# Loading two weight matrices in two halves each, in a linear-attention and mixture layer on eight cores

## What is computed

```python
xn = layernorm(x)
# attention branch: linear attention with decay, 8 heads of 64
q, k = phi(xn @ W_Q.T), phi(xn @ W_K.T)          # phi(u) = elu(u) + 1
v    = xn @ W_V.T
S = g*S + outer(k_t, v_t);  z = g*z + k_t        # scan over 2048 steps
y = (S.T q_t) / (z.q_t + eps) * sigmoid(xn @ W_g_w.T + W_g_b)
# other branch: a linear layer and two of eight rank-4 adapters by softmax weight
base = xn @ W_lin.T + b_lin
lora = sum over top-2 e of score_e * (xn @ left_e) @ right_e
out  = x + y @ W_O.T + base + lora
```

## Time and profile before

| What | us |
|---|---|
| Median of the timed runs (2 runs, 416.75 and 417.91) | 417.33 |
| The profiled execution: its time | 418.39 |
| The profiled execution: span of its slowest core, core 7 | 417.3 |
| Busy on core 7: TensorE matmuls | 311.7 |
| Busy on core 7: VectorE | 204.0 |
| Busy on core 7: ScalarE | 131.2 |
| Busy on core 7: GpSimd | 24.6 |

### The profile page before, as it was taken

One profiled execution on the slowest core, in us unless ns is written; L12 is line 12 of the kernel. 1 busy time (PEld: TensorE's weight loads), 2 busy tenths in 40 slices (PEclk: granted clock), 3 DMA queues, 4 the chain that ended last, 5 costly groups with the idle time before them and its releaser, 6 DMA issues.

```text
span 417.3 us, 6496 instructions; the slowest of 8 cores (407.2 to 417.3 us)
## 1 busy us (share of the span) xinstructions
PE 311.7 (75%) x2066; PEld 142.6 (34%) x2066; DVE 204.0 (49%) x807; ACT 131.2 (31%) x281; POOL 24.6 (6%) x64
## 2 busy tenths in 40 slices
PE   0002797417999989368999987379999896799966
PEld 0002342202344534233444443224444444244421
DVE  5040175205267616364665456455575276555741
ACT  1827133474143224416225234150223141401100
POOL 0910000210000000120000000200000002000000
PEclk9999998665699999759999999589999996799977
DMA  7999998000033321000320110001011100010111
GB/s 197 230 211 154 155 164 138 2 0 1 0 103 102 101 61 41 2 1 2 101 87 20 49 52 0 3 0 49 2 53 52 50 1 2 0 52 2 50 52 50
DMA packets 12850, 24.95 MB, mean 60 GB/s; under 512 B 2929, under 2 KB 7153, under 8 KB 12818
## 3 DMA queue, kind: packets, MB, share of 16 engines
q0 software_dynamic: 7856, 7.49, 12.9%
q1 hardware_dynamic: 4242, 14.43, 10.5%
q10 hardware_dynamic: 720, 2.62, 2.0%
HBM read 23.63 MB, written 8.39 MB: 77 GB/s over the span
## 4 chain that ended last, share of the span: by engine, by line
PE 65%; ACT 10%; DVE 9%; issue 7%; POOL 6%; DMA 2%; DVEq 1%; ACTq 0%; SPq 0%; POOLq 0%
PE pQK L786 15%; PE pG L584 8%; PE pQK L799 8%; PE pQK L400 7%; PE pA L400 4%; PE pG L400 3%; PE pV L572 3%; PE pQK L790 3%; PE pT L340 2%; PE pQK L793 2%; ACT gsig L591 2%; DMA crow_s<-crow 2%; PE pO L572 2%; ACT scr1b L286 2%; DVE A_sb L628 2%
## 5 line engine op out<-in xcount | busy, mean ns | idle before, releaser
L786 PE MATMUL pQK<-wlin_sb,xnfm 128*128 128x512 bf16 x256 | 66.1, 405 | 4.8 <-DVE th_sb L557 4.7
L808 DVE TENSOR_TENSOR out_sb<-pQK,x_sb 128x512 f32<-128x512 f32 x32 | 22.1, 692 | 78.6 <-PE pQK L799 75.0
L584 PE MATMUL pG<-wg_sb,xnfm 128*128 128x512 bf16 x128 | 36.0, 432 | 17.1 <-DVE den_r L729 16.2
L591 ACT ACTIVATE gsig<-pG 128x512 bf16<-128x512 f32 x16 | 9.6, 598 | 100.6 <-PE pG L588 100.6
L786 PEld LDWEIGHTS pQK<-wlin_sb,xnfm 128*128 128x128 bf16 x256 | 24.9, 103 | 33.9 <-issue 12.4
L799 PE MATMUL pQK<-wo_sb,ygfm 128*128 128x512 bf16 x128 | 34.9, 397 | 0.0
L415 ACT ACTIVATE phir<-phiw 128x512 bf16<-128x512 f32 x32 | 19.9, 630 | 33.0 <-DVE phiw L409 33.0
L737 DVE SCALAR_TENSOR_TENSOR ygtm<-gsig,den_r,pA 128x64 bf16<-128x64 bf16 x128 | 26.0, 276 | 4.4 <-issue 3.8
L584 PEld LDWEIGHTS pG<-wg_sb,xnfm 128*128 128x128 bf16 x128 | 13.2, 106 | 37.4 <-issue 25.9
L628 DVE TENSOR_TENSOR A_sb<-pA,masks 128x128 bf16<-128x128 f32 x64 | 17.9, 280 | 11.0 <-PE pG L615 11.0
L340 PE MATMUL pT<-ident_s,xn_tm 128*128 128x128 bf16 x128 | 10.9, 241 | 15.0 <-ACT xn_tm L325 12.9
(11 more groups left out here) (144 smaller groups left out, 507.3 us busy)
## 6 DMA issues: line engine op xcount, KB each, us to landing
out<-out_sb SPq DMA_DIRECT2D x16, 512.0 KB, 2.7
x_sb<-x SPq DMA_DIRECT2D x11, 512.0 KB, 5.7
x_sb<-x ACTq DMA_DIRECT2D x5, 512.0 KB, 11.5
wlin_sb<-wlin POOLq DMA_DIRECT2D x1, 2048.0 KB, 49.4
wq_sb<-wq POOLq DMA_DIRECT2D x1, 1024.0 KB, 19.9
wk_sb<-wk POOLq DMA_DIRECT2D x1, 1024.0 KB, 26.4
wv_sb<-wv POOLq DMA_DIRECT2D x1, 1024.0 KB, 32.0
wg_sb<-wg POOLq DMA_DIRECT2D x1, 1024.0 KB, 37.1
```

Of the source, the lines that this page charges most:

```text
L584: TE.matmul(pG[:, :], xnfm[:, 1024 * k + cs * 128 : 1024 * k + cs * 128 + 128], wg_sb[:, FH * k : FH * k + FH], start=(k == 0), stop=False)
L786: TE.matmul(pQK[bank][:, :], xnfm[:, 1024 * k + cs * 128 : 1024 * k + cs * 128 + 128], wlin_sb[:, D * k + 512 * n : D * k + 512 * n + 512] ...
L808: ins = VE.tensor_tensor(out_sb[:, cp * D + 512 * n : cp * D + 512 * n + 512], pQK[bank][:, :], x_sb[:, cx * D + 512 * n : cx * D + 512 * ...
```

## The change

The DMAs of `wv` and `wg` are each issued as two DMAs of four slabs. The second halves have semaphores of their own, "v2" and "g2". In `E_vg` TensorE waits for these before the matmul of k = 4, in every call.

```diff
-    s_wg = {g: nc.alloc_semaphore(f"s_w_{g}") for g in ["qk", "k2", "v", "g", "lg", "ow", "wo2"]}
+    s_wg = {g: nc.alloc_semaphore(f"s_w_{g}")
+            for g in ["qk", "k2", "v", "v2", "g", "g2", "lg", "ow", "wo2"]}
...
-            (wq_sb, wq_d, "qk"), (wk_sb, wk_d, "k2"), (wv_sb, wv_d, "v"),
-            (wg_sb, wg_d, "g"), (wlin_sb, wlin_d, "ow"), (wo_sb, wo_d, "wo2")]
+            (wq_sb, wq_d, "qk", None), (wk_sb, wk_d, "k2", None),
+            (wv_sb, wv_d, "v", "v2"), (wg_sb, wg_d, "g", "g2"),
+            (wlin_sb, wlin_d, "ow", None), (wo_sb, wo_d, "wo2", None)]
...
+        else:
+            h_ = kk // 2
+            dv = dst[:, :].rearrange("p (k c) -> p k c", k=kk)
+            sv = srcd.rearrange("k p c -> p k c")
+            GP.dma_start(dv[:, 0:h_, :], sv[:, 0:h_, :]).then_inc(s_wg[grp], 16)
+            GP.dma_start(dv[:, h_:kk, :], sv[:, h_:kk, :]).then_inc(s_wg[grp2], 16)
+            w_tot[grp] += 16
+            w_tot[grp2] += 16
...
         for k in range(KCH):
+            if k == KCH // 2:
+                TE.wait_ge(s_wg["v2"], w_tot["v2"])
             ins = TE.matmul(pVb[:, :],
...
         for k in range(KCH):
+            if k == KCH // 2:
+                TE.wait_ge(s_wg["g2"], w_tot["g2"])
             TE.matmul(pG[:, :],
```

More of the change, by code:

```diff
@@ L175, in build_core @@
                                      ALU.subtract))
-    wmap = [(gatew_sb, gatew_d, "lg"), (left_sb, left_d, "lg"),
-            (wq_sb, wq_d, "qk"), (wk_sb, wk_d, "k2"), (wv_sb, wv_d, "v"),
-            (wg_sb, wg_d, "g"), (wlin_sb, wlin_d, "ow"), (wo_sb, wo_d, "wo2")]
+    wmap = [(gatew_sb, gatew_d, "lg", None), (left_sb, left_d, "lg", None),
+            (wq_sb, wq_d, "qk", None), (wk_sb, wk_d, "k2", None),
+            (wv_sb, wv_d, "v", "v2"), (wg_sb, wg_d, "g", "g2"),
+            (wlin_sb, wlin_d, "ow", None), (wo_sb, wo_d, "wo2", None)]
     w_tot = {g: 0 for g in s_wg}
-    for dst, srcd, grp in wmap:
+    for dst, srcd, grp, grp2 in wmap:
         kk = srcd.shape[0]
-        GP.dma_start(dst[:, :].rearrange("p (k c) -> p k c", k=kk),
-                     srcd.rearrange("k p c -> p k c")).then_inc(s_wg[grp], 16)
-        w_tot[grp] += 16
+        if grp2 is None:
+            GP.dma_start(dst[:, :].rearrange("p (k c) -> p k c", k=kk),
+                         srcd.rearrange("k p c -> p k c")).then_inc(s_wg[grp], 16)
+            w_tot[grp] += 16
[5 more added lines that the diff above has]
+            GP.dma_start(dv[:, h_:kk, :], sv[:, h_:kk, :]).then_inc(s_wg[grp2], 16)
+            w_tot[grp] += 16
+            w_tot[grp2] += 16
     GP.dma_start(right_sb[:, :], right_d[:, :]).then_inc(s_wg["ow"], 16)
```

## The result

The changed kernel takes 420.33 us (median of 13 runs), the kernel before 416.87 (12 runs beside them). The ratio is 1.0084, 95% interval 1.0062 to 1.0106, so the change costs 3.5 us, between 2.6 and 4.4. That is within 2%, and inside the range, but about three times the 1.2 us of the forecast. Where do the other 2.3 us come from? Some executions of this program fall into a second, slower state whatever the kernel (one of 456.49 us here), and the ratios, means and shares in this document leave those out.

A forecast was written before the change was run, and what follows sets the result against it. The prediction took TensorE's stream and its hand-overs to ScalarE and VectorE as the bound. To the median of 417.33 us it added 1.22 for GpSimd's issues and 0 for the rest: 418.5 us, range 415.2 to 420.8.

The forecast's parts named there:

- Earlier start of V and G: First V and G projections: `wv` and `wg` already land 13.7 and 10.5 us before use, so gain 0.
- Two more issues: GpSimd's queue ahead of `tcol`: two half issues cost 1.48 instead of 0.87 us per matrix, together +1.22 us, on the path.
- Landings covered: Weight loads at the start: second halves land 0.6 and 1.2 us later, still covered by over 9 us.
- The waits: Inside TensorE's V and G groups: 32 more waits cost 0 each; upper end 0.04 us each, 1.3 us.
- The rest of the kernel runs as before but 1.22 us later: Everything behind the first `tcol`: delayed once by +1.22 us, otherwise unchanged.
- the granted clock falls into other places: Clock-dependent stretches on all cores: a 1.2 us shift changes what they meet; 410.1, about 415.1, or 417 to 418.5; chance 0.13.
- Its sign: TensorE's busy time on the slowest core, 311.7 us: a change by several us would be the clock.
- The full queue: GpSimd's DMA queue at the start: a limit of eight under way would stall the last issues; 432 us, chance 0.03.
- the hidden issue: GpSimd's issues ahead of `tcol`: cheap halves or later ScalarE statistics let less than 1.2 us through; 417.3 to 417.6, chance 0.08.

The follow-up runs named there:

- e3: Kernel before with four small GpSimd operations ahead of the first `tcol`, no split and no added wait: 417.62 us, ratio 1.0022.
- e5: Kernel before with five small GpSimd operations ahead of the first `tcol`, no split and no added wait: 417.42 us, ratio 1.0003.
- e8: Kernel before with ten small GpSimd operations ahead of the first `tcol`, no split and no added wait: 419.18 us, ratio 1.0038.
- e1: Kernel before with only the 32 waits inside the V and G groups, no DMA split: 418.04 us, ratio 1.0028.
- e11: Kernel before with one small GpSimd operation behind `init_tail()`, where GpSimd is idle: 418.05 us, ratio 1.0023.
- e10: Changed kernel with two small GpSimd operations more behind `init_tail()`, where GpSimd is idle: 419.16 us, ratio 1.0052 against the kernel before.
- e12: Changed kernel with `wlin`, `wo` and `right` issued behind `nlg_lo` and two small GpSimd operations more: 417.85 us, ratio 1.0016 against the kernel before.
- e7: The changed kernel measured again, nothing altered: 420.77 us, ratio 1.0069 against the kernel before.
- e4: Kernel before with the DMAs of `wlin`, `wo` and `right` issued behind `tcol` and `nlg_lo`: 415.71 us, ratio 0.9973.
- e2: Changed kernel with the split kept, but the second-half waits only once each, ahead of the first chunk's groups: 419.84 us, ratio 1.0079 against the kernel before.
- e6: Changed kernel with the DMAs of `wlin`, `wo` and `right` issued behind `tcol` and `nlg_lo`: 418.99 us, ratio 1.0041 against the kernel before.
- e9: Kernel before with two small GpSimd operations behind `init_tail()`, where GpSimd is idle: 418.95 us, ratio 1.0055.

## Why the prediction was right or wrong

**The number: inside the range by luck.** 420.33 lies in 415.2 to 420.8, but not in 417.5 to 419.5, the range of the forecast itself. The upper end was made of waits at 0.04 us each and of halves as dear as wholes (420.4), and neither happened.

**Earlier start of V and G, 0: right.** No TensorE wait names either matrix.

**Two more issues, +1.22 us, all on the path: right**, and its working too. The halves took 0.73 to 0.74 us each, `gatew` to `tcol` 9.00 us against the 9.0 forecast, and e3, e5 and e8 show at equal clock that a later `tcol` is paid in full. The rule weighed beside it, from the Trainium skill (DMA: Bandwidth & Descriptors, Anatomy of one DMA), is that descriptor generation is small and many can be emitted before it shows. A half as dear as a whole would have made the sum 1.74; the trace, with 1.24, sides with the row of `wo`.

**Landings covered: right.** `wq` was put at 35.0 us and landed at 37.1; it kept 9.2 us.

**The waits, 0: right as far as the runs tell.** e1 is 0.3 us over at equal clock with an error of 0.1 to 0.2, far below the 1.3 us of the upper end. e11, which has no wait, is 0.3 over as well.

**"The rest of the kernel runs as before but 1.22 us later": this is the step that failed.** Two terms were missing from the sum. The first is a stall of 0.35 us at 264 us, on TensorE's path through `tcol`, `varn`, `nmrc`, `ktm_sb`, which two more instructions on GpSimd set off 240 us later. With it the sum at equal clock is 1.2 + 0.35 = 1.6; measured is 1.7 to 1.9, and the 0.1 to 0.3 left over are within what e1's waits and the error allow. The second is the clock. The mean fell from .910 to .900 or .901, which at 3.2 us for each 0.01 is about 3 us on the mean of the cores: 415.9 - 411.0 = 4.9 us, of which 1.8 are at equal clock and 3.1 clock. The time itself grew only by 3.5, since it is that of the slowest of eight, and in 54 of the 83 compared runs of before the slowest core had the dear clock already, 416.4 us on average, where after has 419.0 in its 12 runs. Of these 2.6 us the 1.8 are at equal clock; the other 0.8 fit with four or five dear cores now instead of one, the slowest of which is slower. In the other 29 runs the slowest core was a cheaper one of 413.8, which adds 0.9 on the mean of all.

**The rival "the granted clock falls into other places" was the right kind and the wrong size.** It saw that middle cores might move to the dear pattern, and gave 417 to 418.5, since they start 0.8 us and more before core 7. In the run after, core 1 did this (`tcol` at 21.15 us, clock 0.894, span 417.4, as that rival has it), but the cores that set the end took more: after `tcol` core 7 needs 419.4 - 21.8 = 397.6 us, where in the earlier trace rows it needs 417.3 - 20.85 = 396.4. The 1.2 us between are the stall and more. And the rival named a shift of the start as what would move the clock, which e3, e5 and e8 refute. Its sign, TensorE's busy time on the slowest core, couldn't show it: 311.7 us before and 310.4 after, since core 7 is dear in both profiles (.894, .898).

**The full queue, and the hidden issue: neither happened.** Eleven issues went through without a pause, and `tcol` follows `right` at once.

**Open.** e1, e10, e11 and e12 have no stall, and still 0.25 to 0.34 of their core spans are dear where before has 0.11. What in such small edits moves the clock, when delays of 1 to 2.3 us don't, these runs don't tell. Of the 3 us of clock, by the shares of e7 and e10 (0.62, 0.34, and 0.11 before), about half goes with the stall; the other half is open. What holds GpSimd's first operation up for 0.35 us at just this place in its stream is open too. No version was shown to be faster than before: e4, with the late issue, is the nearest, 0.9973 with an interval of 0.9941 to 1.0004.

## What to carry to other kernels

Splitting a DMA is not free on the engine that issues it: price each issue by a row of the same number of rows, and ask whether a compute operation stands behind it in that queue. Any added instruction also shifts everything behind it in that engine's stream, and can cost at a place that has nothing to do with the edit, so compare the two traces over the whole span, above all the first operation behind each long wait. On a kernel whose cores differ by clock, compare spans at equal clock and the clock by itself; the slowest core's time mixes the two.

## What the runs showed of the hardware

- GpSimd's first operation after an idle time of 78 us starts 0.11 to 0.12 us after its wait is through, and 0.44 to 0.47 us after it where the stream is two instructions longer, on all eight cores (after, e2, e6, e7, e9). Two more instructions undo it (e10, e12). A packet of the instruction queue follows `tcol`'s start with it (after) and without it (before).
- TensorE's mean clock over eight cores rose when this stall was taken out (.900 to .905 from e7 to e10, .900 to .908 from e6 to e12) and didn't react to a start 2.3 us later (.911 in e8). Small edits without a stall move it as well (.910 to .906 in e11). 0.01 of mean clock is worth 2.9 to 3.5 us of this kernel's 411.
- A semaphore wait that is already met, inside a group of eight matmuls, leaves the group's 1.89 us as it is (the first G group, in after and in e1).
